# Three stages of a mixture-of-experts layer put into one block of engine programs

## The reference, cut to what matters

```python
def _mlp(x, gw, uw, dw):
    return jax.nn.silu(x @ gw.T) * (x @ uw.T) @ dw.T
...
rw = _route(x, gate_w, gate_bias)          # [4096, 64], 8 weights a token are not zero
expert_out = jax.vmap(lambda gw_, uw_, dw_: _mlp(x, gw_, uw_, dw_))(Wg, Wu, Wd)
routed = jnp.einsum('eth,te->th', expert_out, rw)
shared = _mlp(x, Sg, Su, Sd)
out = (routed + shared).reshape(B, S, H)
```

## Time and profile before

| | us |
|---|---|
| three runs | 1688.82, 1688.90, 1694.95 |
| median | 1688.9 |
| profiled execution | 1688.62, of which its span is 1686.9 |

### The profile page before, as it was taken

The page is one execution under the profiler, slowest core; times in us unless marked ns, Lnnn a source line. Parts: engine busy times, 40 slices in busy tenths (PEclk is TensorE's granted clock), DMA queues, the critical chain, the costliest instruction groups (busy, mean ns, idle before and its releaser), DMA issues. The chain is left out here.

```text
span 1686.9 us, 43323 instructions
## 1 busy us (share of the span) xinstructions
PE 1356.2 (80%) x16876; PEld 996.6 (59%) x16876; DVE 1238.0 (73%) x2062; ACT 937.0 (56%) x1418; POOL 838.6 (50%) x851
## 2 busy tenths in 40 slices
PE   4588887538859999989957899873588699999798
PEld 1243433324439999978823455532344499999677
DVE  2477876697846777779945888828888377777898
ACT  4434342527747777743241766663477577777322
POOL 5356464406744444447753555432177344444575
PEclk9889998859979999989985999997599799999899
DMA  2353535004446777757713222100054477777576
GB/s 73 108 175 126 175 127 200 1 1 177 197 164 176 208 205 212 208 164 211 212 41 94 78 72 80 37 1 1 26 206 192 146 209 205 211 207 209 170 230 203
DMA packets 201853, 241.85 MB, mean 143 GB/s; under 512 B 16006, under 2 KB 139832, under 8 KB 201528
## 3 DMA queue, kind: packets, MB, share of 16 engines
q1 hardware_dynamic: 176055, 155.18, 30.1%
q0 software_dynamic: 25600, 83.91, 14.8%
HBM read 110.57 MB, written 128.45 MB: 142 GB/s over the span
## 5 line engine op out<-in xcount | busy, mean ns | idle before, releaser
L932 POOL TENSOR_TENSOR moe_exp_hl<-moe_exp_h,moe_exp_hh 88x512 f16<-88x512 f32 x184 | 212.1, 1153 | 288.1 <-ACT moe_exp_hh L903 155.5
L811 PE MATMUL psum<-moe_exp_xT,gu 128*88 128x128 f16 x1472 | 260.9, 220 | 1.4 <-issue 0.6
L812 PE MATMUL psum<-moe_exp_xT,gu 128*88 128x128 f16 x1472 | 260.7, 220 | 0.0
L813 PE MATMUL psum<-moe_exp_xT,gu 128*88 128x128 f16 x1472 | 260.7, 220 | 0.0
L890 ACT ACTIVATE moe_exp_xT<-psum 128x1024 f16<-128x1024 f16 x184 | 188.2, 1024 | 125.0 <-PE psum L846 125.0
L752 POOL DMA_INDIRECT x_table<-moe_send_sent,moe_row x160 | 154.5, 966 | 149.7 <-ACT moe_send_sent L682 92.9
L912 DVE SCALAR_TENSOR_TENSOR moe_exp_h<-psum,moe_exp_h 88x512 f32<-88x512 f32 x184 | 126.3, 687 | 135.2 <-ACT moe_exp_h L897 100.2
L811 PEld LDWEIGHTS psum<-moe_exp_xT,gu 128*88 x1472 | 177.1, 120 | 3.8 <-issue 1.9
L813 PEld LDWEIGHTS psum<-moe_exp_xT,gu 128*88 x1472 | 177.6, 121 | 0.0
L812 PEld LDWEIGHTS psum<-moe_exp_xT,gu 128*88 x1472 | 177.5, 121 | 0.0
L682 ACT ACTIVATE moe_send_sent<-psum 128x1024 f16<-128x1024 f32 x128 | 130.2, 1020 | 75.5 <-PE psum L640 52.3
(11 more groups left out here) (393 smaller groups left out, 3938.0 us busy)
## 6 DMA issues: line engine op xcount, KB each, us to landing
moe_exp_xg<-x_table SPq DMA_DIRECT2D x184, 256.0 KB, 3.2
y_table<-moe_exp_y SPq DMA_DIRECT2D x184, 256.0 KB, 2.6
x_table<-flow_zero SPq DMA_DIRECT2D x96, 256.0 KB, 5.2
qk_scratch<-attn_parts SPq DMA_DIRECT2D x48, 128.0 KB, 2.4
y_table<-flow_zero SPq DMA_DIRECT2D x16, 256.0 KB, 4.2
attn_q_st<-qk_scratch SPq DMA_DIRECT2D x16, 256.0 KB, 2.9
attn_k_st<-qk_scratch SPq DMA_DIRECT2D x16, 256.0 KB, 3.3
flow_wg_stage<-in_wg_dram SPq DMA_DIRECT2D x8, 352.0 KB
```

Of the source, the lines that this page charges most:

```text
L811: pe.matmul(out, a_hi, b_hi, start=True, stop=False)
L812: pe.matmul(out, a_hi, b_lo, start=False, stop=False)
L813: return pe.matmul(out, a_lo, b_hi, start=False, stop=True)
L932: pool.tensor_tensor(hl[m % 3][:], h[m % 3][:], hh[m % 3][:], ALU.subtract).then_inc(hl_ready, 1)
```

## The change

`dispatch`, `experts` and `combine` become one function with one block, `moe_layer`, called twice. Inside a layer there is now no barrier, no branch and no DRAIN between the three; what the barriers ordered is ordered by semaphore waits that were put between the parts on each engine: SP waits for all scatters to have landed (`written`) before its first load; PE, ACT, DVE and POOL wait for the last use of what they will overwrite; POOL waits for all stores (`stored`) before its first fetch. The wait for `written` on POOL now stands behind the experts' part. The buffers of `experts` and `combine` are no longer their own but lie over buffers that are spent (`xw`, `xh`, `xl`, `sent`, `pick`). And the first tables of the summing, those of the first pair's tails and of the first two blocks, are computed by TensorE in step 93 of the experts' loop, between down(90) and down(91), instead of at the head of `combine`. The number of DMAs, matmuls and vector operations is the same.

```diff
 
 
-def dispatch(nc, g, tag):
+def moe_layer(nc, g, tag, out_dram):
...
+
+        def on(tensor, at, n, shape, dtype=F16):
+
...
+        xg = on(spent, 0, 4, [P, RUN * 2 * D])
+        y = [a.rearrange("p (i h d) -> p i h d", h=2, d=D) for a in on(spent, 4 * RUN * 2 * D, 4, [P, RUN * 2 * D])]
+        hr = on(g.xh[:], 0, 3, [INNER, TILE], F32)
+        hr_hi = on(g.xl[:], 0, 3, [INNER, TILE])
+        hr_lo = on(g.xl[:], 3 * TILE, 3, [INNER, TILE])
+        xT = [sb(f"xT{k}", [P, 2, P, RUN], F16) for k in range(3)]
+        ps_T, ps_gate2, ps_up2, ps_out = ([g.bank[2 * k], g.bank[2 * k + 1]] for k in range(4))
+        (turned, xT_ready, gate_done, up_done, run_silu_done, run_h_ready, run_hh_ready, run_hl_ready, run_down_done, y_ready) = (
+            sem(n) for n in ("turned", "xT_ready", "gate_done", "up_done", "run_silu_done", "run_h_ready", "run_hh_ready",
+                             "run_hl_ready", "run_down_done", "y_ready"))
...
+        weight = picked[:, 2 * RUN * 4 * P:2 * RUN * 4 * P + 8 * P].rearrange("p (b h t) -> p b h t", h=2, t=2 * P)
+        weight_t = g.xl[:, 6 * TILE:6 * TILE + 2 * P].rearrange("p (h t) -> p h t", h=2)
+        unit = g.xl[:, 6 * TILE + 2 * P:6 * TILE + 4 * P].bitcast(F32)
+        ps_tail = g.bank[0]
+        ps_block = [g.psum[:, 512:1280], g.psum[:, 1536:2304]]
+        ps_sum = [g.bank[5 + k][:, 0:P] for k in range(3)]
+        tail_made, block_made, tail_copied, block_copied, tail_back, block_back, tail_summed, summed, sum_added, out_stored, unit_made = (
+            sem(n) for n in ("tail_made", "block_made", "tail_copied", "block_copied", "tail_back", "block_back",
...
+        def _(sp):
+            for k in range(6):
+                sp.wait_ge(written[k], 16 * ((K - k + 5) // 6))
+            sp.wait_ge(rows_ready, K)
+            def load(s):
+                sp.dma_start(xg[s % 4][:], g.x_table[s * P:(s + 1) * P, :]).then_inc(loaded[s % 4], 16)
+
...
+            for k in range(4):
+                sp.wait_ge(stored[k], 16 * (G // 4))
+            if out_dram is not None:
+                for n in range(NTILES):
+                    at = slice(n * TILE, (n + 1) * TILE)
+                    sp.wait_ge(sum_added, NSUB * (n + 1))
+                    sp.dma_start(out_dram[:, at], g.x_res[:, at]).then_inc(out_stored, 16)
+                sp.wait_ge(out_stored, 16 * NTILES)
 
         @block.tensor
...
+            pe.wait_ge(pick_ready, NSUBS)
+            wait_sent(pe, K - 2)
+            wait_sent(pe, K - 1)
+            pe.wait_ge(sent_act, (SLOTS - 1) * PAIRS)
+            pe.wait_ge(silu_done, units)
+            pe.wait_ge(h_ready, units)
+            pe.wait_ge(added, NTILES)
...
+                if s == G + 1:
+                    pe.wait_ge(xT_ready, G)
+                    tail_tables(0)
+                    pe.wait_ge(run_silu_done, G)
+                    block_tables(0)
+                    pe.wait_ge(run_h_ready, G)
+                    block_tables(1)
+                if 1 <= s < G:
+                    address_in(s, (2, 3))
+            pe.wait_ge(y_ready, G)
+            for q in range(PAIRS):
...
+            act.wait_ge(gate_up, units)
...
+            act.wait_ge(rows_ready, K)
...
-            for k in range(6):
-                pool.wait_ge(written[k], 16 * ((K - k + 5) // 6))
...
-            tail_tables(0)
-            block_tables(0)
-            block_tables(1)
...
+            dve.wait_ge(turned, G)
...
+            pool.wait_ge(gate_up, units)
+            for m in range(G):
...
+            pool.wait_ge(turned, G)
+            for k in range(6):
+                pool.wait_ge(written[k], 16 * ((K - k + 5) // 6))
+            for k in range(4):
+                pool.wait_ge(stored[k], 16 * (G // 4))
+            def fetch(out, q, slot):
...
                 routing(nc, g, f"{tag}_route")
-                dispatch(nc, g, f"{tag}_send")
-                experts(nc, g, f"{tag}_exp")
-                combine(nc, g, f"{tag}_sum", out_dram)
+                moe_layer(nc, g, f"{tag}_run", out_dram)
```

More of the change, by code:

```diff
@@ L607, in _, with tables @@
         @block.tensor
         def _(pe):
+            def tables(out, n, b, at, half):
+                own = g.owner[half, b // 2, at]
+                pe.matmul(out[:, 0:P], own, g.place[half, b // 2, :], start=True, stop=False)
+                pe.matmul(out[:, 0:P], g.minus4[half, at], g.ones16[half, :], start=False, stop=True)
+                pe.matmul(out[:, n:n + P], own, g.w_hi[half, b // 2, :], start=True, stop=True)
+                return pe.matmul(out[:, 2 * n:2 * n + P], own, g.w_lo[half, b // 2, :], start=True, stop=True)
@@ new lines, in _, with read, address_in @@
+            into, out_of = [None] * G, [None] * G
+            def read(m):
+                _, at[m] = nc.values_load_multi_w_load_instructions(
+                    g.expert[0:1, 8 * m:8 * m + 8], engines=[mybir.EngineType.PE], min_val=0, max_val=(EXPERTS - 1) * D,
+                    skip_runtime_bounds_check_because="the table holds min(count, EXPERTS - 1) times a width")
+                into[m] = [None] * 4
+            def address_in(m, tiles):
+                for i in tiles:
+                    into[m][i] = [part(g.gu[k], at[m][2 * i].with_bounds(min_val=0, max_val=(EXPERTS - 1) * INNER), INNER) for k in range(4)]
+                    for w in into[m][i]:
+                        pe.lower_ap(w, for_matmul_weights=True)
@@ new lines, in _ @@
+            for q in range(PAIRS):
+                act.wait_ge(tail_made, q + 1)
+                if q >= 1:
+                    act.wait_ge(tail_back, q)
+                act.activation(weight_t[:], ps_tail[:, P:3 * P].rearrange("p (k t) -> p k t", k=2), ACT.Copy).then_inc(tail_copied, 1)
+                copy_block(2 * q)
+                if q == 0:
+                    act.activation(unit[:], g.ident[:], ACT.Copy, scale=TS * YS).then_inc(unit_made, 1)
+                else:
+                    take(2 * q - 2)
+                copy_block(2 * q + 1)
+                if q >= 1:
+                    take(2 * q - 1)
@@ L693, in _ @@
+            take(NSUBS - 2)
+            take(NSUBS - 1)
         @block.vector
@@ L907, in _ @@
+            dve.wait_ge(rows_ready, K)
             for s in range(G + 4):
```

463 lines of the change are left out of this document (188 added, 275 removed).

## The result

The changed kernel takes 1684.67 us (median of 20 runs, 1679.34 to 1690.70), the kernel before 1690.09 (median of 20, 1684.06 to 1696.53). The ratio is 0.9961, with a 95% interval of 0.9950 to 0.9973: 0.4% faster, 6.6 us. The forecast was 1687.0, "same" with a chance of 0.73. The number is right, but two of the terms behind it are not, and one term that counts is missing, as will be seen.

A forecast was written before the change was run, and what follows sets the result against it. Bounds: POOL's 6.6 us DRAINs at the first place and layer's end, POOL's fetches in combine. From 1688.62, layers win 0.75 and 1.2, giving 1686.7; 0.3 more to match the median gives 1687.0 us, range 1678.5 to 1691.

The forecast's parts named there:

- first place: Between dispatch and experts: SP waits for `written` itself instead of behind POOL's DRAIN, first load 6.85 us sooner per layer.
- clock: First groups of experts: TensorE still at its lower clock after less idling; counted 0, bound 2.5 us less.
- second place: Between experts and combine: POOL waits for `stored` itself, fetch 1.0 us sooner; net -0.5 each after the tables' cost.
- down(91) behind the tables: End of experts: 24 table matmuls before down(91) make DVE's last half, store and fetch 0.53 us late per layer.
- tables made early, gain: Start of combine: first pair's selecting matrices ready 3 to 4 us sooner, buying nothing; counted 0, 1 us a layer either way.
- fetches of `combine`: In combine: POOL sets the pace at 1.251 us a fetch, and the change leaves that pace untouched.
- DRAIN at the layer's end: End of each layer: POOL's DRAIN follows 160 indirect DMAs and takes 13.2 us instead of 6.6.
- I take the price for each: POOL's DRAIN: 0.082 us for each indirect DMA since the last DRAIN, like a list being walked; chance 0.65.
- is not a wait for bytes: POOL's DRAIN: 6.59 us whether its 80 DMAs had landed or the last were under way, so not set by landing.
- paid in part: Rival, layer's end: POOL strikes off finished scatters or holds only so many, half the added 6.6 gone; 1680.4 us, chance 0.15.
- fixed price: Rival, POOL's DRAIN: 6.6 us after indirect DMAs whatever their number, each layer wins 7.35; 1674.2 us, chance 0.15.
- the bound of +0.2: Second place: worst net change per layer, if the tables run at the lower clock and take twice their 1.35 us.

The follow-up runs named there:

- drain_old_5: Changed kernel plus one POOL DRAIN in combine, behind 80 old scatters and 5 fetches (first layer) or 20 (second); these DRAINs took 7.10 and 8.23 us; no total time given.

## Why the prediction was right, and where it wasn't

| term, both layers together | forecast | profile |
|---|---|---|
| first place, from last scatter to first load | -13.7 | -14.0 |
| from TensorE's first matmul to the first store, clock | 0 | -0.6 |
| groups of `experts`, reads of the table | not in the sum | +5.1 |
| second place, POOL's own wait instead of the barrier | -2.0 | -0.5 |
| down(91) behind the tables | +1.1 | +1.2 |
| tables made early, gain | 0 | 0 |
| fetches of `combine` | 0 | 0 |
| DRAIN at the layer's end | +13.2 | +0.8 |
| sum | -1.4 (-2.0 in the forecast, since there the output ends the second layer) | -8.0 |

**The first place** was right in mechanism and size: 6.85 forecast, 7.0 measured, with the load's own landing next.

**"I take the price for each"** was right: 0.082 us for each, shown at 60, 75, 80, 85 and 100. That the DRAIN "is not a wait for bytes" is right for these lengths; for 20 and 40 it is in part one. **"The DRAIN behind it takes 160 x 0.082 = 13.2"** is the step that failed. The count doesn't add up over the block; of 160 only 85 are paid. Of the three readings on the list, "paid in part" came closest in mechanism, with 6.2 of the added 6.6 gone instead of half. Of the two reasons that I gave for it, that POOL strikes off finished scatters while it waits between the `hl` is wrong: 250 us later all 80 are still there. That it "holds only so many" is nearer, but no single number fits (100 paid, then 65). The argument against it, that an even pace of the fetches means no books kept on the way, failed: the pace is as even as before and 75 entries are gone. The argument against a fixed price, that 80 was the only count in the trace, was sound.

**What hid this error** is a term that stood nowhere. By the DRAIN alone, the time would have been 12.4 us lower (13.2 forecast, 0.8 measured), near the fixed price's 1674.2. Of that the groups of `experts` took back 5.1. I had followed the order of the instructions on every engine, found it unchanged in `experts`, and took its length as unchanged. But the merge also puts the buffers of `experts` over xw, xh and xl, and that is a change of the code in `experts` too. I gave it no line and no bound. Nor was the place forced: `pick` and `sent` are free by then, as the later kernels with xg and y over them show.

**The second place**: forecast -0.5 a layer, measured +0.14 and +0.57 in the profile. POOL takes 0.8 us from its last wait to the first fetch in both kernels: its wait is over at 740.1, the fetch starts at 740.88. I had counted on the fetch right behind the wait, though the row of before has the barrier at 746.7 and the fetch at 747.49. The tables' price was forecast at 0.53, and is 0.38 in the first layer and 0.82 in the second, where down(91) ran at the lower clock; the bound of +0.2 for that was too narrow (net +0.57).

**The clock** was, as taken, at its lower level when the first groups began. Over 490 to 507.5 the granted clock is 0.78 instead of 0.51, but that stretch now begins 8 us further on in the work. From TensorE's first matmul it is 3.8 us to the 2.4 GHz level in both layers after. Before, it was 5.6 in the first layer and 3.8 in the second. After, first layer, and before, second layer (first matmuls at 493.89 and 1333.20):

```profile
490.00:507.50 17.50, 12.92 (x195) 12.35 (x195) 4.53 (x7) 9.90 (x15) 3.46 (x3) 0.78 0.50 151
497.70:507.50 9.80, 9.43 (x167) 9.19 (x165) 4.04 (x6) 7.90 (x13) 3.46 (x3) 1.00 0.34 95
```

```profile
1336.98:1346.00 9.02, 8.71 (x156) 8.59 (x155) 3.59 (x6) 7.17 (x11) 3.37 (x3) 1.00 0.39 97
```

That gave 0.8 us up to the first store in the first layer, and -0.1 in the other, within the bound of 2.5. The shorter idle stretch (4.1 us instead of 11.8) isn't shown to be its cause: before, the second layer had 11.1 us of idling and rose after 3.8, and the second layer of `drain_old_5` had 4.7 and rose after 5.9.

**The sum.** The profile says -8.0 from the last scatter to the end of the last DRAIN, where the medians say -5.4 and the ratio -6.6 (4.6 to 8.5): they agree as well as single executions do, whose times spread over 11 to 12 us in either kernel. That the result lies within 2.4 us of the forecast is luck: a DRAIN was 12.4 us too dear on paper, with 5.1 us in `experts` and 1.6 at the second place too cheap. The range of 1678.5 to 1691 was taken from the right uncertainty, how much of the list is paid; the forecast's value wasn't.

## What to carry to other kernels

Buffers laid over others to merge two stages change the later stage even when not one instruction of it moves: compare the durations of small reads and address work in that stage, and try another placement before calling the merge done. POOL's DRAIN at a block's close costs by the count of indirect DMAs since the last one (0.082 us each here), whether they are long finished or not; if POOL has idle time that nobody waits on, put a DRAIN there, and don't assume that counts of several stages add up. Work moved ahead of the last step of a stage is paid by those who wait for that step (0.4 us here, and more where the clock fell on it), so move it only if somebody waits for what it makes.

## What the runs showed of the hardware

- A read of SBUF into a TensorE register (TENSOR_LOAD) takes 0.80 to 0.83 us on average with y over `sent` or in tiles of its own, and 0.93 to 0.94 with y in either half of xw (means of the middle 80 groups of a layer). That held in all 28 layers of the 14 profiles, on chips of either pace. The groups are 0.02 to 0.04 us longer each with the slow read (the layer with a DRAIN between two groups left out).
- POOL's DRAIN costs 0.082 us for each indirect DMA since the last one (60 to 100 of them); behind 20 and 40 it is longer than that, with 0.04 for each behind the landing of the last one. Of 80 old scatters all are paid for with 20 fetches behind them, and five with 40 to 80.
- One chip had the same two programs 7 to 8% slower. The changed kernel's fetches came 1.8 us apart there, since POOL waited for buffers, where the first chip had 1.25, bound by POOL's issues.
